# First cell of a sixteen-cell convolution grid: 32-row products in ordered phases

## The chip, the cores and the metric

One NeuronCore of a Trainium2 chip runs the whole program. The metric is the time of one execution on the device in microseconds (us), from the first to the last instruction; lower is better. Engines are named as in the profile: PE (TensorE) multiplies matrices into PSUM banks, ACT (ScalarE) and DVE (VectorE) do the elementwise work, POOL (GpSimd) does little here, SP issues the DMAs. The kernel before took 3323.1 us, the median of two runs (3318.69 and 3327.51).

## The reference

The input is 8 images of 16 channels, 112 x 112, float32. Four residual blocks follow one another; each adds to the stream what it computes from the group-normalised stream (8 groups of 2 channels, over a whole image).

- Block 0: attention of single-channel heads inside 4 x 4 windows, between two 16 x 16 projections.
- Block 1: a 3 x 3 convolution, 16 to 16 channels.
- Block 2: a grid of 4 columns by 4 rows of cells. A cell is a 3 x 3 convolution of one to three 16-channel inputs (right neighbour's output, output from below, output from above), a bias and a ReLU. It gives up to three 16-channel outputs: RIGHT, UP, DOWN.
- Block 3: a 3 x 3 convolution of values quantised with one scale over all images.

```
for col in range(4):
    for row in range(4):
        if col == 0: ins = [x] if row == 0 else [outs[row-1][DOWN]]
        elif ...                                   # two or three inputs
        outs[row] = relu(conv3x3(concat(ins), W[col,row]) + b[col,row])   # split in three
return outs[3][RIGHT]
```

The first cell, (0, 0), reads the normalised stream alone. Only its DOWN and RIGHT outputs are used.

## The kernel before

**Layout.** An image is held as pairs of rows: 16 channels x 2 rows make 32 partitions, and the 56 row pairs lie along the free dimension. A 3 x 3 convolution of a row pair also needs the row above and the row below; these neighbour rows are kept as 32 further partitions, copied by DMA (the halo, `send_half`, `send_pair`). A cell with a single input reads a "half" tile `S[k]`: 128 partitions are two image halves h of 64, and each 64 are 32 of own rows and 32 of neighbour rows. A two-input cell reads a "pair" tile `P[r]`, all 128 partitions of it in one product. `w_all` holds the weights, 32 columns for each of the three horizontal taps kx.

**Units.** An output of a cell is made in two units, u = 0 and 1. A unit is a product of 32 output partitions by 392 columns (`QN`) in 8 places: four column quarters q (PSUM partitions 32q) in two PSUM banks. `conv_unit` (from L781) writes units alternately to banks 0 and 1 and to banks 2 and 3 of `conv_banks` (`unit_banks`). Products of pair tiles are L800 (128 rows x 32 columns of the array, four side by side), those of half tiles L813 (64 x 32, eight side by side: four quarters q, two halves h). Every product in the code shows in the trace as two float32 MATMUL rows with a LDWEIGHTS each, so the 24 products of L813 in a unit show as x48. A unit ends with one increment of `conv_done`.

**Order.** Each engine has its program order; semaphores tie them. A PE unit k waits until unit k - 2, which had the same two banks, is emptied (`relu_done` by ACT, `vec_relu_done` by DVE):

```
pe.wait_ge(relu_done, unit_base(m) + k - 1)
if k >= 2 and units_in(m)[k - 2][0] in shared_in(m):
    pe.wait_ge(vec_relu_done, vec_value(m, k - 2))
```

ACT empties units in order (`empty`, L662). Cells in `SHARED_MID` and `SHARED_LATE`, the first cell among them, are emptied half by ACT (q = 0, 1) and half by DVE (q = 2, 3; L985). DVE has the attention of a later image in between; it takes the shared cells at fixed places of its list, the first cell after step 4 of the attention, and stands still until their units are made. An emptied output's halo is sent by SP.

**Staging.** The grids of successive images overlap: `BODY` lists 16 cells, 68 units, of which six cells belong to the image before. The first cell is the fifth of the list, units 14 to 17 (DOWN 0, DOWN 1, RIGHT 0, RIGHT 1), after cell (2, 3) and before cell (3, 2), both of pair products. `body(-1)` has only the early cells and begins with the first cell; there ACT empties all of it. `body(0)` to `body(4)` are a hardware loop, `body(5)` and `body(6)` stand written out, `body(7)` has no first cell. So the first cell is made eight times.

Of the kernel before, what the change touches and what calls it, by code (L numbers as in the profile page):

```python
# [42 lines left out]
RIGHT, UP, DOWN = 0, 1, 2  # L43


NQ = 4
QG = G // NQ
QX = W // NQ
QN = QG * QX
# [9 lines left out]
def has_pair(col, row):  # L59
    return col > 0  # L60


def has_single(col, row):
    return col == 0 or 0 < row < ROWS - 1
# [19 lines left out]
def in_places(col, row):  # L84

    if col == 0:
        return [INPUT if row == 0 else out_place(0, row - 1, DOWN)]
    got = [("pair", row, 0), ("pair", row, 1)]
    return got + ([out_place(col, row - 1, DOWN)] if has_single(col, row) else [])


def single_place(col, row):
    return in_places(col, row)[-1]


def strips_of(col, row, u):
    return (u, u + 2) if has_single(col, row) else (2 * u, 2 * u + 1)
# [9 lines left out]
def units_of(body):  # L107
    return [(cell, o, u) for cell, late in body for o in cell_outs(*cell) for u in range(2)]
# [7 lines left out]
def body_of(m):  # L116
    return (EARLY_BODY if m < 0 else LATE_BODY if m == B - 1 else BODY) if isinstance(m, int) else BODY


def units_in(m):  # L120
    return units_of(body_of(m))


def unit_base(m):

    return 0 if isinstance(m, int) and m < 0 else m * NB + NF
# [87 lines left out]
def shared_in(m):  # L214
    return {-1: SHARED_FIRST, B - 2: SHARED_LATE, B - 1: SHARED_LAST}.get(m, SHARED_MID) if isinstance(m, int) else SHARED_MID


def n_shared(m, end):
    return sum(cell in shared_in(m) for cell, _, _ in units_in(m)[:end])


def vec_value(m, k):

    ahead, per = n_shared(-1, NF), sum(cell in SHARED_MID for cell, _, _ in UNITS)
    if not isinstance(m, int):
        return m * per + ahead + n_shared(m, k + 1)
    if m < 0:
        return n_shared(m, k + 1)
    return ahead + min(m, B - 2) * per + (n_shared(B - 2, NB) if m == B - 1 else 0) + n_shared(m, k + 1)


def sides(m, first, mid, before, late={}, last={}):

    return {-1: first, B - 3: before, B - 2: late, B - 1: last}.get(m, mid) if isinstance(m, int) else mid


W_PAIR, W_SINGLE, _n = {}, {}, 0
# [9 lines left out]
def conv_block(nc, x, wqkv, wproj, bproj, rel_bias, w1, wc, bc, w3, sw3, b3, g_all, ident, out):  # L247
    ctx = ExitStack()
    with ctx:
        def sb(name, shape, dt=FP32):  # L250
            return ctx.enter_context(nc.sbuf_tensor(name, shape, dt))

        def sem(name):
            return ctx.enter_context(nc.semaphore(name))
# [10 lines left out]
        S = [sb(f"half{k}", [128, HG, XP]) for k in range(3)]  # L265
# [3 lines left out]
        w_all = sb("w_cells", [128, W_ALL])  # L269
# [39 lines left out]
        conv_ps = ctx.enter_context(nc.psum_tensor("conv_banks", [128, 4, 512], FP32))  # L309
# [20 lines left out]
        def first_sum(kind, j):  # L330
# [7 lines left out]
             for t in range(2)]  # L338
# [12 lines left out]
        conv_done = sem("conv_done")  # L351
        relu_done = sem("relu_done")
        vec_relu_done = sem("vec_relu_done")
# [8 lines left out]
        held = sem("held")  # L362
        sp_held = sem("sp_held")
        pe_held = sem("pe_held")
        norm_sems = [{n: sem(f"{n}{k}") for n in ("meanvar_ready", "mean_done", "spread_ready",
                                                  "var_done", "base_ready", "rstd_done", "norm_ready")}
                     for k in range(4)]
# [37 lines left out]
        def wait_halos(eng, m, what, kinds=("pair", "half", "input")):  # L405
            for key, value in halo_values(m, what):
                if key[0] in kinds:
                    eng.wait_ge(halo[key], value)

        def unit_banks(k):  # L410
            return 2 * (k % 2)
# [289 lines left out]
        def _(pe):  # L701
# [72 lines left out]
            def conv_unit(m, k, cell, o, u, first):  # L774
                row = cell[1]
                n = unit_banks(k)
                if first:
                    wait_halos(pe, m, cell, ("pair",))
                if not (isinstance(m, int) and m < 0 and k < 2):
# [4 lines that stand above are left out]
                if cell == LAST:  # L784
                    for kx in range(3):
                        w = w_all[:, W_PAIR[cell, o] + 32 * kx:W_PAIR[cell, o] + 32 * kx + 32]
                        for b in range(2):
                            at = QX * (2 * u + b) + kx
                            for s in range(NQ):
                                done = nc.tensor.matmul(conv_ps[32 * s:32 * s + 32, n + b, 0:QN], w,  # L790
                                                        P[row][:, QG * s:QG * (s + 1), at:at + QX],
                                                        start=kx == 0, stop=kx == 2)
                    return done
                strips = strips_of(*cell, u)
                single = has_single(*cell)
                for kx in range(3) if has_pair(*cell) else []:
                    w = w_all[:, W_PAIR[cell, o] + 32 * kx:W_PAIR[cell, o] + 32 * kx + 32]
                    for b, s in enumerate(strips):
                        for q in range(NQ):
                            done = nc.tensor.matmul(conv_ps[32 * q:32 * q + 32, n + b, 0:QN], w,  # L800
                                                    P[row][:, QG * s:QG * (s + 1), QX * q + kx:QX * (q + 1) + kx],
                                                    start=kx == 0, stop=kx == 2 and not single)
                if single and first:
                    wait_halos(pe, m, cell, ("half",))
                if single and (first or not has_pair(*cell)):
                    pe.sem_inc(pe_held, 1)
                T = S[single_place(*cell)[1]] if single else None
                for kx in range(3) if single else []:
                    at = W_SINGLE[cell, o] + 32 * kx
                    for q in range(NQ):  # L810
                        for h in range(2):
                            rows = slice(64 * h, 64 * h + 64)
                            done = nc.tensor.matmul(conv_ps[32 * q:32 * q + 32, n + h, 0:QN], w_all[rows, at:at + 32],  # L813
                                                    T[rows, QG * u:QG * (u + 1), QX * q + kx:QX * (q + 1) + kx],
                                                    start=kx == 0 and not has_pair(*cell), stop=kx == 2)
                return done

            def body(m):
                seen = None
                for k, (cell, o, u) in enumerate(units_in(m)):  # L820
                    for kind, j, d in sides(m, PE_FIRST, PE_MID, PE_BEFORE).get(k, []):
                        side_step(m + d, kind, j)
                    if cell == (0, 0) and cell != seen:
                        wait_halos(pe, m, "input")
                    conv_unit(m, k, cell, o, u, cell != seen).then_inc(conv_done, 1)
                    seen = cell

            pe.wait_ge(consts_in, N_CONST * 16)
# [34 lines left out]
            pe.wait_ge(zeroed, N_ZERO)  # L863
            pe.wait_ge(w_in, 16)
            body(-1)
            with pe.Fori(0, B - 3) as m:
                body(m)
            body(B - 3)
            body(B - 2)
            body(B - 1)  # L870
# [7 lines left out]
            for s in range(28):  # L878
# [5 lines left out]
                for q in range(6):  # L884
                    T, dx = (Q, QH)[q // 3][t], q % 3
                    done = nc.tensor.matmul(conv_ps[:, s % 4, 0:4 * W], w3b[:, q * 128:(q + 1) * 128],  # L886
                                            T[:, g:g + 4, dx:dx + W], start=q == 0, stop=q == 5)
# [450 lines left out]
```

## Time and profile before

| | |
|---|---|
| runs | 3327.51 and 3318.69 us, median 3323.1 us |
| profiled execution | span 3324.9 us (first to last instruction; nothing lies around it) |
| busy | PE 2919.7 us (88%), DVE 2272.9 (68%), ACT 2042.5 (61%), POOL 23.2 (1%) |
| chain that ended last | PE 71%, DVE 10%, ACT 8%, issue 7% |
| the chain by line | L800 41%, L813 19%, L833 5%, L662 (pair) 4%, L662 (half) 3% |

Busy time of PE is the union of its matmul rows; these run up to eight side by side, and their ends are modelled. The chain is followed back from the last instruction: at each step to the work that released it. A timeline row merges neighbouring instructions of one group: start, length, engine, line, count; in brackets stands the idle time of the engine before it and what ended that.

### The profile page before, as it was taken

To read this page: it belongs to the slowest core of one execution; us is meant where nothing else is said; L and a number is where in the kernel's file an instruction comes from. 1 tells how busy PE (TensorE), PEld (TensorE's weight loads), DVE (VectorE), ACT (ScalarE), POOL (GpSimd) and SP (SyncE) were. 2 spreads that over 40 slices of the span, in tenths; PEclk is the share of its full clock that TensorE was granted. 3 is DMA by queue.
4 is the path that set the end of the run, shared out by engine and by line. 5 is a ranking of instruction groups with operands and counts; after the bars stand their busy time and mean duration, and the time that the engine had idled before them with its cause. 6 is when DMAs were issued, how large, how long until landed. Compare 5 with 4: busy or idle time off the path is not lost.

```text
span 3324.9 us, 87852 instructions
## 1 busy us (share of the span) xinstructions
PE 2919.7 (88%) x39580; PEld 1250.6 (38%) x39580; DVE 2272.9 (68%) x1998; ACT 2042.5 (61%) x2317; POOL 23.2 (1%) x67
## 2 busy tenths in 40 slices
PE   5775699998999899989999899989998989999944
PEld 5774233333333333333333333333333333333312
DVE  6565996689858894989678985889498941320224
ACT  1010887586767666667757676776676665767413
POOL 0000000000000000000000000000000000000000
PEclk9887899999999999999999999999999999999977
DMA  3012557566665766576766666676667565775566
GB/s 59 0 10 29 69 76 89 77 88 97 80 91 73 109 79 81 75 96 94 89 79 89 98 79 90 78 104 75 88 79 98 85 84 65 94 108 76 66 125 120
DMA packets 95703, 269.69 MB, mean 81 GB/s; under 512 B 79824, under 2 KB 80592, under 8 KB 83408
## 3 DMA queue, kind: packets, MB, share of 16 engines
q1 hardware_dynamic: 95312, 263.86, 59.2%
q8 instruction: 320, 5.24, 0.9%
q14 instruction: 71, 0.58, 0.1%
HBM read 23.01 MB, written 12.85 MB: 11 GB/s over the span
## 4 chain that ended last, share of the span: by engine, by line
PE 71%; DVE 10%; ACT 8%; issue 7%; SPq 1%; DMA 1%; POOL 0%; DVEq 0%; ACTq 0%; POOLq 0%
PE conv_banks L800 41%; PE conv_banks L813 19%; PE conv_banks L833 5%; ACT pair L662 4%; ACT half L662 3%; PE side_banks L728 2%; DVE half L985 2%; PE side_banks L761 1%; DVE pair L985 1%; PE stat_bank L771 1%; DVE score_max L1008 1%; ACT scores L648 1%; PE conv_banks L886 1%; DVE scores L1000 1%; DVE scores L998 1%
## 5 line engine op out<-in xcount | busy, mean ns | idle before, releaser
L662 ACT ACTIVATE pair<-conv_banks,b_cells 32x784 f32<-32x784 f32 x1316 | 1235.7, 939 | 604.8 <-PE conv_banks L813 539.7
L800 PE MATMUL conv_banks<-pair,w_cells 128*32 128x392 f32 x17664 | 1554.7, 501 | 40.2 <-issue 26.1
L813 PE MATMUL conv_banks<-half,w_cells 64*32 64x392 f32 x18432 | 894.4, 513 | 145.0 <-ACT pair L662 64.1
L800 PEld LDWEIGHTS conv_banks<-pair,w_cells 128*32 128x32 f32 x17664 | 539.0, 109 | 999.2 <-issue 937.3
L662 ACT ACTIVATE half<-conv_banks,b_cells 32x392 f32<-32x392 f32 (+1 forms) x780 | 528.8, 678 | 200.9 <-PE conv_banks L813 139.0
L813 PEld LDWEIGHTS conv_banks<-half,w_cells 64*32 64x32 f32 x18432 | 335.0, 107 | 685.2 <-issue 651.9
L985 DVE TENSOR_SCALAR half<-conv_banks,b_cells 32x392 f32<-32x392 f32 (+1 forms) x180 | 114.4, 636 | 334.7 <-PE conv_banks L813 178.7
L985 DVE TENSOR_SCALAR pair<-conv_banks,b_cells 32x784 f32<-32x784 f32 x220 | 227.5, 1034 | 113.6 <-PE conv_banks L813 103.2
L998 DVE TENSOR_TENSOR scores<-qkv 128x1792 f32<-128x1792 f32 x106 | 214.1, 2020 | 105.9 <-ACT qkv L643 105.7
L648 ACT ACTIVATE scores<-scores 128x1792 f32<-128x1792 f32 x106 | 180.1, 1699 | 76.0 <-DVE scores L1010 74.1
L1008 DVE TENSOR_REDUCE score_max<-scores 128x112 f32<-128x1792 f32 x106 | 214.1, 2020 | 9.8
L1000 DVE TENSOR_TENSOR scores<-scores,rel_bias_sb 128x1792 f32<-128x1792 f32 x106 | 214.6, 2025 | 3.6
L1010 DVE TENSOR_TENSOR scores<-scores,score_max 128x1792 f32<-128x1792 f32 x106 | 214.6, 2025 | 3.6
L1024 DVE TENSOR_TENSOR scores<-scores,qkv 128x1792 f32<-128x1792 f32 x98 | 198.4, 2025 | 3.4
L1027 DVE TENSOR_REDUCE score_max<-scores 128x112 f32<-128x1792 f32 x98 | 197.9, 2020 | 3.4
L1022 DVE TENSOR_REDUCE softmax_sum<-scores 128x112 f32<-128x1792 f32 x98 | 197.2, 2012 | 1.4 <-ACT scores L648 0.5
L643 ACT ACTIVATE qkv<-side_banks 128x672 f32<-128x672 f32 x56 | 41.0, 732 | 228.4 <-PE side_banks L761 105.8
L833 PE MATMUL conv_banks<-scores,pair 128*128 128x112 f32 x512 | 102.7, 375 | 23.6 <-DVE att L1062 21.1
L833 PEld LDWEIGHTS conv_banks<-scores,pair 128*128 128x128 f32 x512 | 99.4, 229 | 26.0 <-issue 22.7
L761 PE MATMUL side_banks<-att,w_qkv_sb 128*128 128x224 f32 x336 | 80.1, 377 | 26.7 <-DVE att L962 26.7
L833 PE MATMUL conv_banks<-pair 128*128 128x112 f32 x384 | 77.0, 376 | 24.9 <-DVE att L1062 24.9
L790 PE MATMUL conv_banks<-pair,w_cells 128*32 128x392 f32 x768 | 68.8, 508 | 30.6 <-issue 29.6
(86 smaller groups left out, 1084.6 us busy)
## 6 DMA issues: line engine op xcount, KB each, us to landing
pair<-pair SPq DMA_DIRECT2D x384, 391.9 KB, 8.6
half<-half SPq DMA_DIRECT2D x352, 192.4 KB, 5.4
x_block<-in_x SPq DMA_DIRECT2D x64, 98.0 KB, 5.5
stream<-in_x SPq DMA_DIRECT2D x64, 98.0 KB, 5.3
x_scratch<-stream SPq DMA_DIRECT2D x8, 784.0 KB, 6.3
pair<-x_scratch SPq DMA_DIRECT2D x8, 784.0 KB, 16.3
out_dram<-pair SPq DMA_DIRECT2D x32, 196.0 KB, 4.2
half<-half SPq DMA_DIRECT2D x176, 7.1 KB, 4.6
```

Source lines behind the costliest of these rows:

```text
L648: nc.scalar.activation(e, e, ACT.Exp).then_inc(exp_done, 1)
L662: done = nc.scalar.activation(dst, src, ACT.Relu, bias=b_ap)
L800: done = nc.tensor.matmul(conv_ps[32 * q:32 * q + 32, n + b, 0:QN], w, P[row][:, QG * s:QG * (s + 1), QX * q + kx:QX * (q + 1) + kx], star ...
L813: done = nc.tensor.matmul(conv_ps[32 * q:32 * q + 32, n + h, 0:QN], w_all[rows, at:at + 32], T[rows, QG * u:QG * (u + 1), QX * q + kx:QX * ...
L833: done = nc.tensor.matmul(first_sum(kind, j), eye, e[:, :, b], start=b == 0, stop=b == WPX - 1)
L985: done = nc.vector.tensor_scalar(dst, src, b_ap, 0.0, ALU.add, ALU.max)
L998: ch.inc(nc.vector.tensor_tensor(e4, q, key, ALU.mult))
L1000: ch.inc(nc.vector.tensor_tensor(e, e, relb[:].unsqueeze(1).to_broadcast([BP, SW, WPX * WPX]), ALU.add))
L1008: ch.inc(nc.vector.tensor_reduce(m[:], ea, AX.X, ALU.max))
L1010: nc.vector.tensor_tensor(ea, ea, row_max(m), ALU.subtract).then_inc(scores_ready, 1)
L1024: side.inc(nc.vector.tensor_tensor(e4, e4, v, ALU.mult))
L1027: side.inc(nc.vector.tensor_reduce(mx[:], ea, AX.X, ALU.add))
```

## The change

The four units of the first cell are no longer made by `conv_unit`. At the first unit of each output (DOWN, RIGHT) PE runs `first_cell_units`, which makes both units u = 0 and 1 of it at once on all four banks. It waits until both earlier units k - 2 and k - 1 are emptied. Each 64-row product is split into a product of the 32 own rows (part 0) and one of the 32 neighbour rows (part 1). For each tap kx there are two phases; in a phase sixteen products, 32 x 32 each, go to sixteen places of the array: 2 parts x 4 quarters x 2 halves. Each of the four 32-row strips (h, part) writes another bank, 2u + h, with u = (phase + part) mod 2; the second phase of a tap swaps the units. After each of the six phases but the last, PE waits on a new semaphore, `part_done`, until the phase's last product is complete. `conv_done` is incremented twice, both in the last phase. The waits of ACT, DVE and SP are as before.

```
--- before.py
+++ after.py
@@ -362,6 +362,7 @@
         held = sem("held")
         sp_held = sem("sp_held")
         pe_held = sem("pe_held")
+        part_done = sem("part_done")
         norm_sems = [{n: sem(f"{n}{k}") for n in ("meanvar_ready", "mean_done", "spread_ready",
                                                   "var_done", "base_ready", "rstd_done", "norm_ready")}
                      for k in range(4)]
@@ -815,6 +816,35 @@
                                                     start=kx == 0 and not has_pair(*cell), stop=kx == 2)
                 return done
 
+            def first_cell_units(m, k, o):
+
+                cell = (0, 0)
+                if not (isinstance(m, int) and m < 0 and k < 2):
+                    pe.wait_ge(relu_done, unit_base(m) + k)
+                    for j in (k - 2, k - 1):
+                        if units_in(m)[j][0] in shared_in(m):
+                            pe.wait_ge(vec_relu_done, vec_value(m, j))
+                pe.sem_inc(pe_held, 1)
+                T = S[single_place(*cell)[1]]
+                for kx in range(3):
+                    at = W_SINGLE[cell, o] + 32 * kx
+                    for phase in range(2):
+                        for part in (1, 0):
+                            u = (phase + part) % 2
+                            for q in range(NQ):
+                                for h in range(2):
+                                    rows = slice(64 * h + 32 * part, 64 * h + 32 * part + 32)
+                                    done = nc.tensor.matmul(
+                                        conv_ps[32 * q:32 * q + 32, 2 * u + h, 0:QN], w_all[rows, at:at + 32],
+                                        T[rows, QG * u:QG * (u + 1), QX * q + kx:QX * (q + 1) + kx],
+                                        start=kx == 0 and phase == 0, stop=kx == 2 and phase == 1)
+                            if kx == 2 and phase == 1:
+                                done.then_inc(conv_done, 1)
+                        if not (kx == 2 and phase == 1):
+                            done.then_inc(part_done, 1)
+                            pe.wait_ge(part_done, (m + 1) * 10 + (5 if o == RIGHT else 0) + 2 * kx + phase + 1)
+                            pe.sem_inc(pe_held, 1)
+
             def body(m):
                 seen = None
                 for k, (cell, o, u) in enumerate(units_in(m)):
@@ -822,7 +852,11 @@
                         side_step(m + d, kind, j)
                     if cell == (0, 0) and cell != seen:
                         wait_halos(pe, m, "input")
-                    conv_unit(m, k, cell, o, u, cell != seen).then_inc(conv_done, 1)
+                    if cell == (0, 0):
+                        if u == 0:
+                            first_cell_units(m, k, o)
+                    else:
+                        conv_unit(m, k, cell, o, u, cell != seen).then_inc(conv_done, 1)
                     seen = cell
 
             pe.wait_ge(consts_in, N_CONST * 16)
```

## Rows read from the trace of the kernel before

**Rows 1.** The page: the span, and the chain of waits by engine.

```profile
span 3324.9 us, 87852 instructions
PE 71%; DVE 10%; ACT 8%; issue 7%; SPq 1%; DMA 1%; POOL 0%; DVEq 0%; ACTq 0%; POOLq 0%
```

**Rows 2.** Windows, first cell, bodies 5 and 6: length, busy by engine, PEclk, DMA.

```profile
2492.44:2503.27 10.83, 8.51 (x195) 3.66 (x192) 6.83 (x10) 10.38 (x14) 0.00 (x0) 1.00 0.60 74
2851.34:2863.02 11.68, 9.34 (x201) 3.59 (x193) 7.08 (x10) 10.58 (x15) 0.00 (x0) 1.00 0.87 104
```

**Rows 3.** Timeline of PE, body 1: start, length, line, count, [idle before].

```profile
1064.33 2.25 PE L813 MATMUL conv_banks<-half,w_cells 64*32 64x392 f32 x48
1068.35 2.25 PE L813 MATMUL conv_banks<-half,w_cells 64*32 64x392 f32 x48 [1.78 <-ACT pair L662]
1070.89 2.25 PE L813 MATMUL conv_banks<-half,w_cells 64*32 64x392 f32 x48 [0.29 <-ACT half L662]
1073.40 2.25 PE L813 MATMUL conv_banks<-half,w_cells 64*32 64x392 f32 x48 [0.26 <-DVE half L985]
1075.58 4.23 PE L800 MATMUL conv_banks<-pair,w_cells 128*32 128x392 f32 x48
```

**Rows 4.** Timeline of ACT, the same stretch.

```profile
1064.42 3.79 ACT L662 ACTIVATE pair<-conv_banks,b_cells 32x784 f32<-32x784 f32 x4 [0.24 <-PE conv_banks L800]
1068.23 4.88 ACT L662 ACTIVATE half<-conv_banks,b_cells 32x392 f32<-32x392 f32 x8
```

**Rows 5.** Timeline of DVE, the same stretch.

```profile
1066.67 2.55 DVE L985 TENSOR_SCALAR half<-conv_banks,b_cells 32x392 f32<-32x392 f32 x4 [7.40 <-PE conv_banks L813]
1070.70 2.55 DVE L985 TENSOR_SCALAR half<-conv_banks,b_cells 32x392 f32<-32x392 f32 x4 [1.48 <-PE conv_banks L813]
1073.29 2.08 DVE L985 TENSOR_SCALAR pair<-conv_banks,b_cells 32x784 f32<-32x784 f32 x2
1075.74 2.08 DVE L985 TENSOR_SCALAR pair<-conv_banks,b_cells 32x784 f32<-32x784 f32 x2 [0.38 <-PE conv_banks L813]
```

**Rows 6.** Timeline of PE, 1068.3 to 1069.0: two rounds of eight.

```profile
1068.35 0.89 PE L813 MATMUL conv_banks<-half,w_cells 64*32 64x392 f32 x16 [1.78 <-ACT pair L662]
```

**Rows 7.** Window from the same start: length, PE busy (count), PEclk, DMA.

```profile
1068.35:1068.41 0.06, 0.06 (x8) 1.00 0.00 0
```

**Rows 8.** Timeline of PE: waits at the start of body 1 and after the cell.

```profile
980.25 1.16 PE L800 MATMUL conv_banks<-pair,w_cells 128*32 128x392 f32 x8 [3.74 <-issue]
...
1092.35 3.32 PE L813 MATMUL conv_banks<-half,w_cells 64*32 64x392 f32 x48 [2.02 <-ACT pair L662]
...
1127.48 5.86 PE L813 MATMUL conv_banks<-half,w_cells 64*32 64x392 f32 x96 [4.47 <-DVE half L985]
```

**Rows 9.** Windows behind such waits, and from the cell to the body's end.

```profile
980.25:984.25 4.00, 4.00 (x28) 1.42 (x32) 3.84 (x3) 0.15 (x1) 0.00 (x0) 0.57 0.55 108
1068.35:1075.58 7.23, 6.68 (x145) 2.80 (x145) 5.43 (x8) 6.51 (x10) 0.00 (x0) 1.00 0.90 113
1092.35:1096.75 4.40, 4.08 (x64) 1.58 (x72) 4.24 (x8) 3.28 (x6) 0.00 (x0) 0.61 0.84 91
1127.48:1131.13 3.65, 3.65 (x48) 1.45 (x56) 2.39 (x4) 0.00 (x0) 0.00 (x0) 0.53 0.09 10
1075.58:1338.70 263.12, 243.94 (x3539) 94.64 (x3532) 208.30 (x191) 177.94 (x201) 1.65 (x3) 0.99 0.71 93
```

**Rows 10.** Timeline of PE at the first cell of body -1.

```profile
331.69 4.09 PE L813 MATMUL conv_banks<-half,w_cells 64*32 64x392 f32 x48 [5.63 <-DMA half<-half]
...
354.27 4.17 PE L813 MATMUL conv_banks<-half,w_cells 64*32 64x392 f32 x48 [4.62 <-DMA half<-half]
```

**Rows 11.** Timeline of ACT at the first cell of body -1.

```profile
335.90 9.72 ACT L662 ACTIVATE half<-conv_banks,b_cells 32x392 f32<-32x392 f32 x16 [2.66 <-PE conv_banks L813]
345.65 3.79 ACT L662 ACTIVATE pair<-conv_banks,b_cells 32x784 f32<-32x784 f32 x4
```

**Rows 12.** Window of the first unit of body -1.

```profile
331.69:335.58 3.89, 3.89 (x49) 1.48 (x56) 3.85 (x3) 1.54 (x1) 0.00 (x0) 0.50 0.00 0
```

## The prediction

> **What bounds the kernel now.** I read the chain of waits first: the product engine PE makes 71% of it [rows 1], so a microsecond that PE loses is lost unless a later wait swallows it. Then the stretch that is edited. The first cell takes 10.83 us in body 5 and 11.68 in body 6, the shortest and the longest of bodies 0 to 6 [rows 2]; I work out body 1 (1064.33 to 1075.58, 11.25 us) and multiply by seven. There PE makes the four units in 2.25 us each, and between them waits 1.78, 0.29 and 0.26 us [rows 3]. What to see: the second unit starts at 1068.35, right after ScalarE (ACT) has emptied the last unit of the cell before (1064.42 + 3.79 = 1068.21) [rows 3, 4], while the first unit ran under that emptying. Products and emptying overlap because a unit holds only two of the four banks. VectorE (DVE) stood idle 7.40 us before it could empty anything of this cell, then empties each unit as it is made [rows 5].
>
> **No product gets cheaper.** 48 matmul rows of pair tiles, four side by side, take 4.23 us; 48 of half tiles, eight side by side, take 2.25 us [rows 3]. A round is thus about 0.35 us whether it holds four products or eight (4.23/12, 2.25/6): only the number of rounds counts. Two units are 96/8 = 12 rounds now. After the change they are six phases of 16 products in two float32 rows each, again 6 x 2 = 12 rounds. Twice the instructions, the same rounds.
>
> **A phase.** Two rounds of eight last 0.89 us from first start to last end [rows 6]; eight products start within 0.06 us, 7 ns apart [rows 7]. Eight more add 8 x 0.007: a phase lasts 0.95 us. Then PE waits for its own last product. No such wait stands in the trace. The nearest row is ACT's end at 1068.21 to PE's start at 1068.35, 0.14 us [rows 3, 4]; I take that, since the way is the same, semaphore to first product. The far end below is no wait at all, when rounds flow on as now: 4.5 us for two units. The far end above is that sixteen don't run at once, priced as a rival. Period 1.09 us, a group of two units 5 x 1.09 + 0.95 = **6.40 us** against 4.50. The register arithmetic for the wait value goes out while the phase's products run; uncovered it would be part of that 0.14. New wait and sixteen-wide issue touch PE's queue alone; behind them stand PE's later cells.
>
> **The banks.** A group takes all four, and this costs most. Step by step in body 1:
> - DOWN can't start at 1064.33; it waits for ACT's end and starts at 1068.35. It ends at 1074.75.
> - DVE and ACT then empty both units. DVE starts 0.09 after PE's end (1064.33 + 2.25 = 1066.58; 1066.67) and needs 2 x 2.55 = 5.10; ACT beside it 4.88 [rows 3, 4, 5]. PE starts 0.14 later: RIGHT at 1080.08, end 1086.48.
> - Cell (3, 2) needs the first RIGHT unit emptied: 0.09 + 2.08 + 0.14 [rows 5]. It starts at **1088.79** instead of 1075.58 [rows 3]: 13.2 us late. The second RIGHT unit is emptied under (3, 2), at no cost: that cell's first unit lasts 4.23 us and more.
>
> Who else is late: DVE leaves the cell at 1086.48 + 0.09 + 2 x 2.08 = 1090.73 instead of 1077.82 [rows 5], 12.9 us; behind these four emptyings stand all its later attention steps and the emptying of later cells. ACT likewise. SP sends the DOWN halo when DVE and ACT are done, about 1080 instead of 1073.3; its reader, cell (0, 1), starts after (3, 2), so that hides, and nothing is added to SP's queue or POOL's.
>
> **The clock.** After waits of 3.74, 2.02 and 4.47 us [rows 8] the granted clock fell to the lower level, 1.2 of 2.4 GHz, for part of the stretch that follows: 0.57, 0.61 and 0.53 on the mean. After 1.78 us it stayed at 1.00 [rows 9]. Each fall costs 4.00 x 0.43, 4.40 x 0.39, 3.65 x 0.47 = 1.7 us. The new waits are 4.02 us (1064.33 to 1068.35), 5.33 and 2.31. I count the first two, 3.4 us, and leave the third, which is near both 1.78 and 2.02, to the range. The Trainium skill (TensorE: Matmul & The Clock Gate, "HAM oscillation") says that a kernel that pauses before every burst of products is throttled anew at each. By that rule the third pause costs too, and the sum would be 12 us higher; the rows leave it open.
>
> **Body -1.** There ACT empties alone: 16 half emptyings 9.72 us, the first four pair emptyings 3.79 [rows 11]. The first unit ran at half clock until 335.58 [rows 12] and took 4.09 us [rows 10], (4.09 - 2.25)/6 = 0.31 more a round, so a phase is 0.95 + 0.62 = 1.57 and its period 1.71. DOWN from 331.69: 2.3 periods to 335.6, 3.7 at 1.09 less the last wait, end 339.5; emptied at 339.6 + 9.7 = 349.3; RIGHT 349.5 to 355.9, with one fall 357.3; first unit emptied 361.2; next cell 361.3 instead of 354.27 [rows 10]. 7 us, between 4 and 10.
>
> **Sum.** 7 x (13.2 + 3.4) + 7 = 123 us. The profiled span is 3324.9 with nothing around it, 1.8 above the runs' median: 3323 + 123 = **3446 us**, +3.7%.
>
> **Rivals.**
> 1. The clock doesn't fall, or falls once: 7 x 13.2 + 5 = 97, **3421** (to 3434). For: 1.78 us did nothing. Against: the three other rows. 0.20.
> 2. The pauses between phases keep it at the lower level through the cell: period 1.71, group 5 x 1.71 + 1.57 = 10.1, so 2 x 3.7 in place of 3.4, and 1.7 at the third: 13.2 + 7.4 + 1.7 = 22.3; x 7 + 9 = 165, **3488**. Against: at 0.26 and 0.29 us of pause in 2.5 it stayed at 1.00 [rows 3, 9], though 0.14 in 1.09 with fewer products at the ends is thinner. 0.12.
> 3. The sixteen don't run side by side (the change would not do what it says): two turns of eight, phase 1.78, group 5 x 1.92 + 1.78 = 11.4, + 10 a body: 13.2 + 10 + 3.4 = 26.6; x 7 + 10 = 196, **3519**. Against: four and eight do. 0.05.
> 4. Sixteen go twice as fast: rounds 0.17, phase 0.61, group 4.36, 4.1 less a body: 7 x 12.5 + 5 = 93, **3416**. Even with products at no cost the cell would end at 1068.35 + 5.33 + 2.31 = 1075.99, later than now. 0.03. The Trainium skill (TensorEngine Tiling (Array Packing), "Theoretical Speedup") gives 2x for dimensions up to 64 and 4x up to 32, which read as a gain from halving the rows would be this rival; equal rounds of four and eight speak against it, since each product then holds half the sum.
> 5. Not slower: PE's delay is swallowed by its later waits. From 1075.58 to the body's end PE is idle 263.12 - 243.94 = 19.2 us [rows 9], the largest 4.47 before 1127.48, released by DVE [rows 8]. If those releases stayed at their times, 16.6 would vanish there and 7 be left: **3330**. It decides at DVE's exit from the cell: on time, the delay is swallowed. But DVE empties the cell itself, and is 12.9 late without the clock's share; ACT's releases hang on PE's units. A fraction swallowed gives times up to 3389. 0.09. Faster than 2% has no mechanism: 0.01.
>
> **Numbers.** Forecast 0.50. The range leaves out rivals 3 and 5: low end 3400 (own wait at nothing, 2 x (6.40 - 4.50) = 3.8 less a body: 7 x 12.8 + 5 = 95, 3418, and without falls of the clock 3394), high end 3495 (rival 2 with a few us); 0.5 + 0.2 + 0.1 + 0.03 lies inside. A 2% difference, 66 us, is about what a measurement here tells from none: slower by more 0.90, within 0.09, faster 0.01.
>
> **What would show it.** In the changed trace: six runs of 32 matmul rows for DOWN, 0.95 us long, 1.09 apart; 5.3 us of PE idle before RIGHT, released by DVE; 2.3 before (3, 2), which starts 13 to 17 us later, counted from the end of cell (2, 3), than now; DVE idle some 15 us ahead of its first emptying of the cell; lower clock behind the first two waits; bodies 0 to 6 each some 16 us longer. Wrong, if periods are near 0.7 or over 1.5, if the loop bodies lengthen much less than the cell, or if the clock stays at 1.00.

## The result and the profile after

The changed kernel takes **3521.9 us** (median of two runs, 3518.82 and 3524.96), 1.060 times the kernel before, 95% interval 1.058 to 1.062: 199 us slower. The profiled execution has a span of 3523.2 us, 198.3 more than before. One kernel below (emptying shared, no shift) had two executions of 6125 and 6206 us at a granted clock of 1.00; its median and ratio leave them out, and their cause is open.

The page of the changed kernel: span, busy times, instruction fetches, chain, the new products (L837):

```profile
span 3523.2 us, 91030 instructions
PE 3004.6 (85%) x41116; PEld 1253.9 (36%) x41116; DVE 2273.6 (65%) x1998; ACT 2040.3 (58%) x2317; POOL 23.2 (1%) x67
...
q8 instruction: 334, 5.47, 0.8%
...
PE 73%; DVE 9%; ACT 8%; issue 7%; SPq 1%; DMA 1%; POOL 0%; DVEq 0%; ACTq 0%; POOLq 0%
...
L837 PE MATMUL conv_banks<-half,w_cells 32*32 32x392 f32 x3072 | 145.8, 744 | 109.5 <-DVE half L1019 37.1
```

PE is busier by 85 us and the chain hangs on it a little more than before [rows 1]. The mean granted clock of the execution fell from 0.955 to 0.926: at two levels, 1.00 and 0.50, that is (1 - 0.926)/0.5 x 3523 = 521 us at the lower one against 299.

Where the time lies, by the first cell of each body (from the end of the unit ahead to the first product behind): the cell takes 35.1, 34.2, 34.1, 35.1, 32.2, 32.3, 32.9 and 33.0 us in bodies -1 to 6 (in body -1 from its first product), against 22.6 in body -1 and 11.2 in each of the other seven. That is 168 us of the 198; 30 lie outside, some 19 of them ahead of the cell in bodies 1 to 4. The timeline of PE at the cell in body 1, to hold against [rows 3]:

```profile
1112.80 0.95 PE L837 MATMUL conv_banks<-half,w_cells 32*32 32x392 f32 x32 [3.98 <-ACT pair L663]
1114.03 1.62 PE L837 MATMUL conv_banks<-half,w_cells 32*32 32x392 f32 x32 [0.28 <-PE conv_banks L837]
1115.85 1.62 PE L837 MATMUL conv_banks<-half,w_cells 32*32 32x392 f32 x32 [0.19 <-PE conv_banks L837]
1117.75 0.99 PE L837 MATMUL conv_banks<-half,w_cells 32*32 32x392 f32 x32 [0.28 <-PE conv_banks L837]
1119.02 0.95 PE L837 MATMUL conv_banks<-half,w_cells 32*32 32x392 f32 x32 [0.28 <-PE conv_banks L837]
1120.25 0.88 PE L837 MATMUL conv_banks<-half,w_cells 32*32 32x392 f32 x13 [0.28 <-PE conv_banks L837]
1123.35 0.91 PE L837 MATMUL conv_banks<-half,w_cells 32*32 32x392 f32 x19 [2.22 <-issue]
1129.50 1.62 PE L837 MATMUL conv_banks<-half,w_cells 32*32 32x392 f32 x32 [5.25 <-DVE half L1019]
1131.40 1.62 PE L837 MATMUL conv_banks<-half,w_cells 32*32 32x392 f32 x32 [0.28 <-PE conv_banks L837]
1133.38 1.62 PE L837 MATMUL conv_banks<-half,w_cells 32*32 32x392 f32 x32 [0.35 <-PE conv_banks L837]
1135.28 1.74 PE L837 MATMUL conv_banks<-half,w_cells 32*32 32x392 f32 x32 [0.28 <-PE conv_banks L837]
1137.25 1.62 PE L837 MATMUL conv_banks<-half,w_cells 32*32 32x392 f32 x32 [0.24 <-PE conv_banks L837]
1139.15 1.62 PE L837 MATMUL conv_banks<-half,w_cells 32*32 32x392 f32 x32 [0.28 <-PE conv_banks L837]
1142.94 6.79 PE L801 MATMUL conv_banks<-pair,w_cells 128*32 128x392 f32 x48 [2.17 <-DVE pair L1019]
```

Five things are to be seen. The waits for the banks are as worked out: 3.98, 5.25 and 2.17 us. A phase is 0.95 us at full clock, but 1.62 at half, and in RIGHT all six are at half. The wait for PE's own product is 0.28, twice what I took. The first unit of cell (3, 2) takes 6.79 us, where it took 4.23 [rows 3]. And one phase is torn in two: 13 rows, then 2.22 us that no semaphore explains, then 19. The last does not belong to the phases alone; the same kind of wait stands twice at the head of the loop, where [rows 8] have it once:

```profile
1407.23 1.11 PE L801 MATMUL conv_banks<-pair,w_cells 128*32 128x392 f32 x6 [3.65 <-issue]
1411.86 3.52 PE L801 MATMUL conv_banks<-pair,w_cells 128*32 128x392 f32 x24 [3.51 <-issue]
```

RIGHT is not at half everywhere. In body 3 its last four phases are back at full clock (the sixth is shown), and the first unit of cell (3, 2) is slow all the same:

```profile
1913.66 0.95 PE L837 MATMUL conv_banks<-half,w_cells 32*32 32x392 f32 x32 [0.28 <-PE conv_banks L837]
1916.78 5.64 PE L801 MATMUL conv_banks<-pair,w_cells 128*32 128x392 f32 x48 [2.17 <-DVE pair L1019]
```

Windows of the two groups of body 1 (length, busy times by engine, PEclk, DMA share, GB/s):

```profile
1112.80:1124.26 11.46, 7.93 (x192) 1.84 (x192) 0.03 (x1) 0.03 (x1) 0.00 (x0) 0.85 0.57 71
1129.50:1140.77 11.27, 9.85 (x192) 1.99 (x192) 0.00 (x0) 0.00 (x0) 0.00 (x0) 0.50 0.46 74
```

DVE, to hold against [rows 5]: it stands still 20.45 us ahead of the cell and 11.45 us inside, and leaves at 1144.99.

```profile
1124.23 5.13 DVE L1019 TENSOR_SCALAR half<-conv_banks,b_cells 32x392 f32<-32x392 f32 x8 [20.45 <-PE conv_banks L837]
1140.80 4.19 DVE L1019 TENSOR_SCALAR pair<-conv_banks,b_cells 32x784 f32<-32x784 f32 x4 [11.45 <-PE conv_banks L837]
```

### The profile page after: what moved, and what is told of

Its sections match the earlier page's. It is cut to its first block, busy times and chain, and to the rows that moved or that the text cites. A ratio compares the mean times of both kernels' runs of the same rounds, so it can differ in the third digit from the quotient of the medians.

```text
span 3523.2 us, 91030 instructions
## 1 busy us (share of the span) xinstructions
PE 3004.6 (85%) x41116; PEld 1253.9 (36%) x41116; DVE 2273.6 (65%) x1998; ACT 2040.3 (58%) x2317; POOL 23.2 (1%) x67
## 4 chain that ended last, share of the span: by engine, by line
PE 73%; DVE 9%; ACT 8%; issue 7%; SPq 1%; DMA 1%; POOL 0%; DVEq 0%; ACTq 0%; POOLq 0%
PE conv_banks L801 40%; PE conv_banks L814 17%; PE conv_banks L867 5%; PE conv_banks L837 4%; ACT pair L663 4%; ACT half L663 3%; DVE half L1019 2%; PE side_banks L729 2%; PE side_banks L762 1%; DVE pair L1019 1%; PE stat_bank L772 1%; ACT scores L649 1%; PE conv_banks L920 1%; DVE score_max L1042 1%; DVE scores L1034 1%
## 5 line engine op out<-in xcount | busy, mean ns | idle before, releaser
L801 PE MATMUL conv_banks<-pair,w_cells 128*32 128x392 f32 x17664 | 1572.3, 505 | 68.6 <-issue 36.3
L814 PE MATMUL conv_banks<-half,w_cells 64*32 64x392 f32 x16896 | 816.4, 512 | 121.5 <-ACT pair L663 55.3
L814 PEld LDWEIGHTS conv_banks<-half,w_cells 64*32 64x32 f32 x16896 | 304.7, 107 | 616.0 <-issue 592.2
L837 PE MATMUL conv_banks<-half,w_cells 32*32 32x392 f32 x3072 | 145.8, 744 | 109.5 <-DVE half L1019 37.1
L837 PEld LDWEIGHTS conv_banks<-half,w_cells 32*32 32x32 f32 x3072 | 31.3, 124 | 220.2 <-issue 219.9
```

The source lines that it names most:

```text
L837: done = nc.tensor.matmul(conv_ps[32 * q:32 * q + 32, 2 * u + h, 0:QN], w_all[rows, at:at + 32], T[rows, QG * u:QG * (u + 1), QX * q + kx: ...
```

## The experiments

I went on with two theories. **A**: the pauses and the long waits hold TensorE at its lower clock, and this is most of what the forecast missed. **B**: fixed prices, the own wait of 0.28 and the waits without a releaser. The rival to both was C, that the split into phases costs and the taking of four banks does not. A further theory, **F**, came from the trace after the first runs: the waits without a releaser are fetches of PE's program. An own wait is PE's wait for its own last product. Ratios are against the kernel before on the same chip, with 95% intervals. The code is shortened, in places to words.

### Four banks at once, 64 rows, no own waits

```
-for phase in range(2):            # 32 x 32, own wait after each phase
+for u in range(2):                # 64 x 32 as before, no own waits
+    for q in range(NQ):
+        for h in range(2): matmul(conv_ps[q, 2*u+h], w_all[64*h:64*h+64], T[64*h:64*h+64, u])
```

> Both units of an output at once on four banks as in the change, but 64-row products as before, no own waits. This is the taking of four banks alone. Theory A and B: 3.98 + 4.4 + 5.25 + 4.4 + 2.2 = 20.2 us and two falls of the clock of 1.7 for the cell, 23.6 in place of 11.25 before: about 3323 + 8 x 12 = 3420 to 3438. Rival C (the split into phases is what costs, the banks are swallowed later): under 3345.

Measured: 3406.3 us, 1.024 [1.022, 1.027]. The taking of the banks alone makes the kernel **82 us** slower; C is out. The timeline of PE at the cell in body 1, and its two groups as windows:

```profile
1078.67 6.75 PE L835 MATMUL conv_banks<-half,w_cells 64*32 64x392 f32 x96 [4.00 <-ACT pair L663]
1090.15 5.90 PE L835 MATMUL conv_banks<-half,w_cells 64*32 64x392 f32 x96 [4.73 <-DVE half L1013]
1097.62 0.87 PE L801 MATMUL conv_banks<-pair,w_cells 128*32 128x392 f32 x8 [1.57 <-DVE pair L1013]
```

```profile
1078.67:1085.42 6.75, 6.75 (x96) 2.45 (x96) 0.55 (x1) 0.55 (x1) 0.00 (x0) 0.61 0.94 119
1090.15:1096.05 5.90, 5.89 (x96) 2.72 (x96) 0.56 (x1) 0.56 (x1) 0.00 (x0) 0.71 0.84 135
```

Without pauses a group runs through and the clock comes back inside it: the fall costs 1.7 us in RIGHT (5.90 x 0.29), which is the price in the forecast, and 2.6 in DOWN (6.75 x 0.39). The wait before RIGHT is 4.73, not 5.25, since the first unit's products end earlier.

### The same with own waits

```
+if kx < 2:                        # phases of one unit and one tap
+    done.then_inc(part_done, 1)
+    pe.wait_ge(part_done, ...)
```

> Both units at once on four banks, phases of sixteen 64-row matmul rows (one unit, one tap) with an own wait after each of the first four, the last two in one run. The pauses of the change without its split into 32 rows. If the pauses hold the clock down, PEclk in RIGHT is 0.5 to 0.6 as in the changed kernel and a cell takes 28 to 31 us, about 3460. If it is the 32-row products, the clock recovers after the first phases: 3.98 + 5.9 + 4.6 + 5.9 + 1.6 = 22 and two falls, 25.4, about 3425.

Measured: 3434.8 us, 1.033 [1.032, 1.035], between the two: four own waits in a group cost 29 us more. The timeline of RIGHT in body 1:

```profile
1104.45 1.56 PE L835 MATMUL conv_banks<-half,w_cells 64*32 64x392 f32 x16 [4.72 <-DVE half L1019]
1106.22 1.56 PE L835 MATMUL conv_banks<-half,w_cells 64*32 64x392 f32 x16 [0.21 <-PE conv_banks L835]
1107.99 1.56 PE L835 MATMUL conv_banks<-half,w_cells 64*32 64x392 f32 x16 [0.21 <-PE conv_banks L835]
1109.75 1.35 PE L835 MATMUL conv_banks<-half,w_cells 64*32 64x392 f32 x16 [0.20 <-PE conv_banks L835]
1111.34 1.55 PE L835 MATMUL conv_banks<-half,w_cells 64*32 64x392 f32 x32 [0.23 <-PE conv_banks L835]
```

The clock stays low over three phases and part of the fourth, 6 us, where RIGHT without pauses spent 2 x 1.7 = 3.4 us there. So in RIGHT pauses lengthen the low stretch with 64 rows too; in DOWN they do not (3.4 to 5.4 us low in bodies 0 to 6, against 3.1 to 5.8 without pauses). With 32 rows it is longer: all six phases of RIGHT are at half in body 1.

### Own waits alone

```
 done = nc.tensor.matmul(...)      # conv_unit, cell (0, 0), two banks a unit
+if cell == (0, 0) and kx < 2:
+    done.then_inc(part_done, 1)
+    pe.wait_ge(part_done, ...)
```

> The kernel before, with an own wait of PE after the first and second tap of each unit of the first cell: own waits alone, two banks a unit and 64 rows as before. A unit is 3 x 0.89 + 2 x 0.28 = 3.2 us in place of 2.25; the short waits of 0.29 and 0.26 go, so the cell is 13.7 in place of 11.25. Theory B: 8 x 2.5 = 20, about 3343. Theory A: the pauses bring the clock down as well, one to two falls of 1.7 us a cell, about 3355 to 3370, with PEclk under 1 in the cell.

Measured: 3347.8 us, 1.008 [1.006, 1.011]. The cell in the profiled execution (an execution of 3336.8 us, at the low end of its runs):

```profile
1064.33:1077.33 13.00, 10.46 (x195) 2.69 (x193) 7.08 (x10) 10.38 (x14) 0.00 (x0) 1.00 0.68 88
```

13.0 us, 1.75 more than before, at PEclk 1.00. Here theory A is wrong: pauses of 0.20 us, twice in each unit, bring no clock down where no long wait stands beside them. Seven cells with this make 12 us, which covers the 10 that the profiled execution lost; what the rest of the median's 25 is was not followed up.

### The loops turned: one own wait in a group

```
-for kx in range(3):
-    for phase in range(2):
+for phase in range(2):
+    for kx in range(3):
...
-    if not (kx == 2 and phase == 1): then_inc(part_done) and wait
+    if kx == 2 and phase == 0: then_inc(part_done) and wait
```

> The changed kernel with its loops turned: all three taps of one phase, one swap, all three taps of the other. The same products, two own waits a cell in place of ten. Theory A (the waits between the phases hold TensorE at the lower clock, and this is most of what the forecast missed): a group is two runs of 2.3 us and one wait, 5.0 us; falls of the clock behind the two long waits only; cell in body 1 some 25 us in place of 34.1, time about 3447. Theory B (the fixed price of the own wait, 0.28 in place of 0.14, and stalls without a releaser that stay): 8 x 0.28 = 2.2 us a cell, about 3504.

Measured: 3465.9 us, 1.044 [1.042, 1.046], between A and B. The timeline of the cell in body 1:

```profile
1094.13 4.13 PE L837 MATMUL conv_banks<-half,w_cells 32*32 32x392 f32 x96 [4.00 <-ACT pair L663]
1098.41 2.74 PE L837 MATMUL conv_banks<-half,w_cells 32*32 32x392 f32 x85
1104.80 1.16 PE L837 MATMUL conv_banks<-half,w_cells 32*32 32x392 f32 x11 [3.65 <-issue]
1108.74 4.15 PE L837 MATMUL conv_banks<-half,w_cells 32*32 32x392 f32 x96 [2.78 <-DVE half L1019]
1113.13 2.89 PE L837 MATMUL conv_banks<-half,w_cells 32*32 32x392 f32 x96 [0.24 <-PE conv_banks L837]
```

The second run of RIGHT as a window:

```profile
1113.13:1116.02 2.89, 2.89 (x96) 1.61 (x96) 0.16 (x1) 0.16 (x1) 0.00 (x0) 1.00 0.52 79
```

Each second run is near full clock, as A says. But at 1.00 it takes 2.89 us, not 2.3: six rounds of sixteen in one run are slower than six of eight (2.25 [rows 3]), which phases of two rounds do not show. And a wait without a releaser of 3.65 us stands in the first group, and as before one more at the loop's head. Counted in the trace of the changed kernel, 2560 and 1280 of PE's instructions (to one or two) lie between the three such waits of body 1 (1024.2, 1123.3, 1173.3); in the kernel before 2048 between the two inside a body: all multiples of 256. The instruction packets in queue q8 are 16384 bytes each, and one ends 1.3 to 1.7 us before PE goes on at each of the three. That is theory F.

### The program shifted

```
+for _ in range(128): pe.sem_inc(pe_held, 1)     # first of all on PE
 pe.wait_ge(consts_in, N_CONST * 16)
```

> The changed kernel with 128 more instructions of PE at its very start, where it waits for data. Theory F (the waits of PE without a releaser are fetches of its program, one every 256 instructions, and hit where such a border falls): the second wait at the loop's head, 4.1 us in bodies 1 to 4, some 15 instructions behind the head, goes; the wait inside the first cell comes 128 instructions, some two phases, earlier. About 3522 - 16 = 3506. If they come from the longer loop as such: unchanged, 3522.

Measured: 3495.9 us, 1.051 [1.050, 1.053]: 26 us less than the changed kernel, more than the 16 expected. The groups of waits without a releaser, of the changed kernel and then of the shifted one (total, times, longest):

```profile
PE conv_banks L801 <- issue: 36.3, 13, 4.9
PE conv_banks L837 <- issue: 15.3, 6, 4.0
PE conv_banks L814 <- issue: 13.2, 8, 2.5
```

```profile
PE conv_banks L801 <- issue: 9.5, 9, 3.3
PE conv_banks L837 <- issue: 14.3, 5, 3.9
PE conv_banks L814 <- issue: 3.6, 2, 3.4
PE conv_banks L801 <- ACT pair L663: 19.5, 6, 4.8
```

The lists do not count alike. In each, two waits of L837 (7.9 us together) are the waits for the banks ahead of the cell in bodies 5 and 6. And the wait at the loop's head, there in both traces, is put down to ACT once in the changed kernel (4.00 us) and four times in the shifted one (17.6, most of the last line). Counted alike, 60.9 us become 37.1, by nothing but the place of the program; in the kernel before they are 38.0. The 24 us are about what the time fell. In bodies 1 to 4 the second wait at the head and the torn phase of DOWN are gone; in body 0 0.52 us stand in RIGHT's last phase. In bodies 5 and 6, where a phase of RIGHT was stretched by 1.6 us before, waits of 2.2 and 3.7 stand in DOWN now. The expectation that the torn phase would move two phases forward failed in the loop bodies. The same shift was given to the turned loops:

> The kernel with the loops turned (one own wait a group), with 128 more instructions of PE at its start. Theory F: the fetch waits of its loop bodies (second wait at the head 2 to 3.7 us, 3.7 in the first cell, 1.8 and 1.3 behind it) go as they did with the changed kernel, about 8 us in each of five bodies, with some 6 us back in the last bodies: 3466 - 35, about 3430, and the kernel with six phases keeps some 60 us over it, the price of four more own waits a group and of the clock that they hold down. If the fetch waits have another cause: 3466.

Measured: 3433.1 us, 1.033 [1.032, 1.035], 33 us less, as F had it. The Trainium skill (Runtime: NRT & Kernel Launch, "Instruction fetch mechanics") describes a program read in blocks of 256 instructions and calls the cost of a border mostly hidden; the borders agree with these counts, the price does not, at up to 2.4 us in the cell and 4.2 at the loop's head in the changed kernel.

### The long waits filled

```
+pe.wait_ge(relu_done, unit_base(m) + k - 1)      # two of four banks free
+24 products of 64 rows into conv_ps[:, 0:2]      # overwritten by the phases
 pe.wait_ge(relu_done, unit_base(m) + k)
```

> The changed kernel, but ahead of each four-bank wait of bodies 0 to 6 PE makes the 24 products of a 64-row unit into the two banks that are free already; the phases overwrite them. Nothing that is waited for comes later, only the idle of PE shrinks (3.98 to 1.8, 5.25 to 2.8 and 0.3). If the long waits bring the clock down: DOWN and most of RIGHT at 1.00, 0.67 us less a phase, some 5 us a body, about 3485. If the pauses between phases do: PEclk as in the changed kernel, about 3522.

Measured: 3508.7 us, 1.058 [1.054, 1.061], 13 less than the changed kernel, though PE has more to do. Windows of the six phases of RIGHT in bodies 0, 1 and 6:

```profile
731.67:739.54 7.87, 6.45 (x198) 1.65 (x192) 0.00 (x0) 0.00 (x0) 0.00 (x0) 0.90 0.63 105
1119.49:1126.68 7.19, 5.85 (x200) 1.66 (x192) 0.00 (x0) 0.00 (x0) 0.00 (x0) 1.00 0.69 112
3023.47:3030.70 7.23, 5.79 (x197) 1.60 (x192) 0.00 (x0) 0.00 (x0) 0.00 (x0) 0.99 0.67 103
```

RIGHT starts right behind the filling products, and five or six of its six phases are at 1.00 in all seven bodies, with the same pauses of 0.28: 7.2 us in place of 11.3. DOWN starts behind a pause of 1.78 us that is left, and there the clock falls in the second phase in six of seven bodies. So neither does it alone: a wait brings the clock down, where pauses follow already one of 1.78 us, which did nothing before dense products [rows 9]; and the pauses decide how long it stays there. The gain on the whole is small because the added products brought fetch waits of 3.9 to 4.9 us into DOWN in three of the bodies.

### A faster kernel

DVE's 7.40 us of idle time [rows 5] ahead of the cell point the other way: not to make the products denser, but to empty sooner what they wait for.

```
+def is_shared(m, cell, o):        # cell (2, 3), RIGHT: emptied half by DVE
+    return cell in shared_in(m) or (0 <= m < B - 1 and (cell, o) == ((2, 3), RIGHT))
-    empty(m, [(0, 0)])            # DVE, after step 4 of the attention
+    empty(m, [(2, 3), (0, 0)])
```

> The kernel before, with the RIGHT output of cell (2, 3), the two units ahead of the first cell, emptied half by VectorE, which stands idle there for 7.4 us. The last unit is emptied at about 1066.5 in place of 1068.2, so the wait of 1.78 us in the first cell shrinks to about 0.1. Own estimate: 1.6 us in bodies 0 to 6, about 3323 - 11 = 3312. If VectorE is late elsewhere for it, no change.

Measured: 3317.5 us, 0.998 [0.997, 0.999]. The cell is 1.5 us shorter in bodies 0 to 6, as expected, 10 us in all; some 5 of them arrive. With shifts of the program:

> The kernel before with the RIGHT output of cell (2, 3) shared, and 64 more instructions of PE at its start. Theory F: fetch waits inside the loop bodies move by 64 instructions of PE; as what hides them there is not known beforehand, between 3305 and 3330.

> The former kernel with 128 more instructions of PE at its start. Theory F: the waits without releaser inside a body (0.41 and 1.81 us in the kernel before) fall elsewhere, where PE waits anyway or not; between 3303 and 3322. The wait at the loop's head stays at 3.7.

> The same with 192 instructions. Theory F: between 3305 and 3330, and another sum of fetch waits in the loop bodies than with 64. If the sums of all shifts are the same, the place of the borders does not matter.

Measured: with 64 instructions **3301.2 us, 0.993 [0.992, 0.995]**; with 128, 3327.4 us, 1.0015 [1.0005, 1.0024]; with 192, 3315.2 us, 0.997 [0.996, 0.998]. The first and the second lie outside what was expected, on either side. The first beats both kernels; a shift of the kernel before alone was not run, so what sharing and shift give apart is known only from the 5 us above. With 192 the loop bodies are as short, but the added instructions delay PE's first unit of the grid by 14 us. With 128 bodies 1 to 4 lose 5 to 7 us ahead of the cell against the kernel before, the changed kernel 4 to 6.5. The timeline with 64:

```profile
1061.26 4.62 PE L818 MATMUL conv_banks<-half,w_cells 64*32 64x392 f32 x96
1066.31 2.25 PE L818 MATMUL conv_banks<-half,w_cells 64*32 64x392 f32 x48 [0.42 <-DVE half L992]
1068.89 2.25 PE L818 MATMUL conv_banks<-half,w_cells 64*32 64x392 f32 x48 [0.33 <-DVE half L992]
```

The wait of 1.78 us between the first two units is gone [rows 3].

## Why the prediction was wrong

The direction was right, the size was not: 123 us forecast, 199 measured, outside the range. Three terms of the sum failed. The largest of them, the fetch of PE's program, was not in it; the clock and the own wait were sized too small.

- **Fetches of the program**: put at nothing, without a reason. "Twice the instructions, the same rounds" took the added instructions to cost only their issue. They moved the borders of the program's blocks to just behind the loop's head and into the cell. In the changed trace torn or stretched phases cost some 17 us in the cells of bodies 0 to 6, and some 19 us are lost ahead of the cell in bodies 1 to 4; a shift of the program alone gave back 26.
- **The clock**: a fall was priced at 1.7 us, from rows in which dense products followed, and two falls were counted. Behind the waits came phases with pauses. RIGHT was at half in all six phases in bodies -1, 0, 1, 2, 5 and 6 and in two phases in bodies 3 and 4; DOWN in two to six. In body 1 that is eight phases x 0.67 = 5.4 us in place of 3.4; by the lengths of the phases some 38 us in bodies 0 to 6 in place of 24. The first unit of (3, 2), left to the range, took 5.6 to 6.8 us in place of 4.23, another 13 us in all, in part made good before the body's end. The prediction's own sign of being wrong, periods over 1.5 us, came in RIGHT (1.9). Rival 2 had this mechanism at 3488 us, and I gave it 0.12; its ground against, that pauses of 0.26 had left the clock at 1.00, holds (own waits alone) but only where no long wait comes first.
- **The rule on pauses ahead of bursts** (the Trainium skill, TensorE: Matmul & The Clock Gate, "HAM oscillation"): its example has waits of 3 to 5 us, so "by that rule the third pause costs too" went further than the page does. The trace decides: in bodies 3 and 4, with RIGHT back at 1.00, (3, 2) still fell behind a pause of 2.17 us. That is a third fall of its own, at 1.4 us.
- **The own wait**: mis-sized. 0.28 instead of the 0.14 of an ACT-to-PE release: 80 waits make 21.4 us, 10 more than forecast. It was 0.20 with 64-row phases and 0.24 in the turned loops.
- **No product gets cheaper**: right. Sixteen products run side by side, and a phase at full clock is 0.95 us, to the hundredth. In one run of six rounds they are even dearer (2.89 against 2.25). Rival 3, whose 3519 us is nearly the measured time, is near it by chance: its phase would be 1.78 at full clock. Rival 4 is refuted by the same row, and with it the reading as a gain of the table in the Trainium skill (TensorEngine Tiling (Array Packing), "Theoretical Speedup").
- **The banks**: right. 3.98, 5.25 and 2.17 against 4.02, 5.33 and 2.31. With the banks alone the time rose by 82 us; the forecast's own figure for groups without own waits, with two falls of the clock, is 95.
- **Nothing swallowed** (rival 5): right in the main. From the cell to the body's end body 1 grew by 1.1 us, though the first unit of (3, 2) alone grew by 2.56; DVE left the cell late, at 1144.99, and with it all later releases.
- **A reading**: the windows of bodies 5 and 6 in [rows 2] are 0.4 us off the cell at one end. The cell takes 11.2 us in all of bodies 0 to 6; the sum, taken from body 1, does not change.

The runs as a ladder: before 3323; banks +82 (3406); split and one own wait, shifted, +27 (3433); four more own waits a group with the clock they keep low, shifted, +63 (3496); fetches +26 (3522). Of the 27, some 19 are the slower runs of sixteen (32 runs x 0.6, an estimate). Of the 63, by the lengths in the traces, some 19 are own waits, some 33 the clock, in the cell and in (3, 2), and some 10 torn phases. Each rung has its own fetch waits, so single rungs are good to some 10 us, not better.

**Open**: why pauses hold the clock down longer with 32-row products than with 64-row ones (0.28 against 0.20 us, or thinner use of the array; not separated); why a run of sixteen-wide rounds is slower than phases suggest; and why a given shift helps or hurts.

## What to carry to other kernels

Before products are packed wider, count the banks that they hold and what can then still be emptied beside them; here that alone cost 82 us, while a round of sixteen products was no faster than one of four or eight. A price for a fall of the clock holds for what follows it: here dense work came back soon, and short phases with own waits stayed low. In a loop body of thousands of PE instructions try a shift of the program before judging a change of one per cent, for here it moved the time by nearly as much.

## What I had not expected of the hardware

- Waits of PE on the fetch of its own program, 0.4 to 5.3 us each, at borders that lie multiples of 256 instructions apart; 128 instructions at the program's start moved the changed kernel by 26 us, and 64 to 192 moved the faster one by 26 us from end to end (3301 to 3327).
- A wait of PE on its own last product took 0.28 us in phases of 32-row products sixteen wide and 0.20 with 64-row ones eight wide, where a release by ACT took 0.14.
- Six rounds of sixteen 32-row products took 2.89 us in one run at a granted clock of 1.00, six rounds of eight 64-row ones 2.25.
- The same six phases with the same pauses ran at 1.00 right behind dense products and at 0.50 behind an idle stretch of 5.25 us.
